# A third transposing bank, mirrors in threes and a regrouped step 0 in a graph-normalisation kernel on one Trainium2 core

## The reference

```python
def adjacent_mat(adj):
    adj = adj + jnp.eye(adj.shape[0])
    deg = jnp.sum(adj, axis=1)
    dinv = jnp.where(deg > 0, deg ** (-0.5), 0.0)
    return dinv[:, None] * adj * dinv[None, :]

S = adjacent_mat((A + A.T) * 0.5)
y = (A @ S) @ x
out = _layernorm(x + y, axis=-1)
```

## Time and profile before

| | us |
|---|---|
| median of 3 runs | 406.44 (406.38 to 407.13) |
| profiled execution, its own time | 406.92 |
| its span, first to last instruction | 405.1 |
| PE busy | 391.6 (97%) |
| DVE busy | 245.4 (61%) |
| ACT busy | 112.5 (28%) |
| POOL busy | 61.0 (15%) |

### The profile page before, as it was taken

How to read it: one execution, slowest core, us unless ns; L and a number is a source line. 1 busy time by engine, 2 the same in 40 slices (tenths; PEclk the granted TensorE clock), 3 DMA queues, 4 the chain that set the end, 5 groups by cost and what they waited for, 6 DMA issues and landing times.

```text
span 405.1 us, 5532 instructions
## 1 busy us (share of the span) xinstructions
PE 391.6 (97%) x1878; PEld 325.5 (80%) x1878; DVE 245.4 (61%) x477; ACT 112.5 (28%) x195; POOL 61.0 (15%) x95
## 2 busy tenths in 40 slices
PE   6989999999999999999999999999999999999994
PEld 5877787878888888888888888888888888888883
DVE  1887888865532622223663357777777778877742
ACT  1245455423332521112222212222222222221200
POOL 3455765732000000000000000000000000000000
PEclk9999999999999999999999999999999999999999
DMA  7999565431026762262322355555655666555300
GB/s 254 342 347 319 155 218 184 136 97 30 0 55 154 170 141 53 52 155 53 104 53 52 93 145 135 147 143 142 155 135 150 155 155 153 145 137 144 95 26 26
DMA packets 67889, 54.76 MB, mean 135 GB/s; under 512 B 3616, under 2 KB 56864, under 8 KB 67872
## 3 DMA queue, kind: packets, MB, share of 16 engines
q1 hardware_dynamic: 67872, 54.54, 50.5%
HBM read 41.94 MB, written 4.19 MB: 114 GB/s over the span
## 4 chain that ended last, share of the span: by engine, by line
issue 72%; PE 18%; DVE 4%; DMA 2%; POOL 2%; SPq 1%; ACT 0%; POOLq 0%; DVEq 0%; ACTq 0%
PE ps L424 4%; PE ps L426 4%; PE ps L425 4%; PE ps L447 3%; PE ps L455 2%; DMA lots_s<-adj 2%; POOL rstd L415 1%; DVE store L687 1%; DVE lots_s L687 1%; DVE c L716 1%; DVE col_acc L711 0%; DVE u_lo L746 0%; PE ps L468 0%; PE ps L436 0%; DVE c_lo L721 0%
## 5 line engine op out<-in xcount | busy, mean ns | idle before, releaser
L670 ACT ACTIVATE w_hi<-store 128x512 fp32r<-128x512 f32 x64 | 39.8, 631 | 122.9 <-DVE store L822 122.9
L424 PE MATMUL ps<-u_hi,w_hi 128*128 128x512 f32 x176 | 69.6, 395 | 0.0
L425 PE MATMUL ps<-u_lo,w_hi 128*128 128x512 f32 x176 | 68.5, 389 | 0.0
L426 PE MATMUL ps<-u_hi,store_lo 128*128 128x512 f32 x176 | 68.5, 389 | 0.0
L822 DVE STREAM_TRANSPOSE store<-store 128x512 f32<-128x512 f32 x64 | 65.5, 1071 | 0.0
L761 DVE SCALAR_TENSOR_TENSOR z_raw<-ps,dinv_half,z_raw 128x512 fp32r<-128x512 f32 x16 | 11.9, 751 | 73.2 <-ACT z_raw L625 73.2
L415 POOL TENSOR_TENSOR rstd<-var_eps,mhalf 128x1 f32<-128x1 f32 x16 | 8.8, 549 | 287.3 <-DVE var_eps L872 287.3
L424 PE MATMUL ps<-z,w_hi 128*128 128x512 f32 x128 | 49.8, 389 | 0.0
L425 PE MATMUL ps<-z,w_hi 128*128 128x512 f32 x128 | 49.8, 389 | 0.0
L426 PE MATMUL ps<-z,store_lo 128*128 128x512 f32 x128 | 49.8, 389 | 0.0
L424 PE MATMUL ps<-store_lo,w_hi 128*128 128x512 f32 x128 | 49.8, 389 | 0.0
(11 more groups left out here) (87 smaller groups left out, 566.5 us busy)
## 6 DMA issues: line engine op xcount, KB each, us to landing
store<-adj SPq DMA_DIRECT2D x65, 256.0 KB, 4.4
u_x<-x SPq DMA_DIRECT2D x16, 256.0 KB, 4.3
z<-z_raw SPq DMA_DIRECT2D x32, 128.0 KB, 2.3
store_lo<-z_raw SPq DMA_DIRECT2D x32, 128.0 KB, 2.3
x_res<-x SPq DMA_DIRECT2D x16, 256.0 KB, 2.6
out<-y_out SPq DMA_DIRECT2D x16, 256.0 KB, 2.0
lots_s<-adj SPq DMA_DIRECT2D x13, 256.0 KB, 4.0
col_slot<-adj SPq DMA_DIRECT2D x6, 448.0 KB, 8.4
```

The costliest lines, as they stand in the source:

```text
L424: nc.tensor.matmul(out_, hi, mov_hi, start=first, stop=False)
L425: nc.tensor.matmul(out_, hi, mov_lo, start=False, stop=False)
L426: return nc.tensor.matmul(out_, lo, mov_hi, start=False, stop=last)
L670: nc.scalar.activation(w_hi2(j)[:, CB * g:CB * g + CB], turned[j][:, CB * g:CB * g + CB], ACT.Copy).then_inc(s_hi2, 1)
```

## The change

- **Banks.** From step 1 on, T alternates between two banks, by a count that runs on over the steps. T(k,i) waits for add(k,i-2) and not for add(k,i-1). Mirrors get a third bank, the one that held the column sums; these keep the last quarter of it. So a mirror has at most three blocks (M counts from the end: 13 to 15, 10 to 12, ...).
- **Column sums.** `col_sums(k)` is now run just before M(k-1,1). ACT copies the result to SBUF (`store_sums`), after the store of M(k-1,1); M(k-1,2) and those behind it wait for that copy too, and so does `degrees(k)`.
- **DVE order.** `lot_low(k-1)` needs the first two mirrors now, and stands behind add(k,1); `u_low(k-1)` stands behind add(k,0). `first_low` 1 to 3 move from steps 2, 3, 4 to steps 5, 6, 8. `rest_high` and `rest_low` of the first rest panel are one step later.
- **Step 0.** Loads come in three parts (blocks 1 to 4, 5 to 11, 12 to 15). Warming transposes are 20, 19 and 20 (before 20 and 36). Column 0 is no longer made by four DVE additions: its blocks are mirrors of row 0, copied by ACT (`store_first`). The clearing of `col_acc` on POOL and the three additions of row 0 to it are replaced by three ACT copies (`first_sum`), one of 128x1280.
- **Loads of steps 1 to 4.** Each row comes in two pieces, the first four blocks early.

```diff
         def mirrors_of(k):
-            parts = [(i, max(b0, k + 1), b1) for i, (b0, b1) in enumerate(chunks_of(k)) if b1 > k + 1]
-            return parts[-1:] + parts[:-1]
+            ends = [(max(b - CB + 1, k + 1), b) for b in range(NB, k + 1, 1 - CB)]
+            return [(next(i for i, (c0, c1) in enumerate(chunks_of(k)) if c0 < b1 <= c1), b0, b1) for b0, b1 in ends]
...
-            return i % 2 if k < 2 else 0
+            return (chunk_at(k) + i) % 2 if k < NR else 0
...
+                for h, (b0, b1) in enumerate(((1, 5), (5, NR), (NR, NB))):
+                    sp.dma_start(c0[:, b0:b1], a_cols[0, :, b0:b1]).then_inc(s_in0[h], 16)
+                    if h == 0:
+                        sp.dma_start(c0[:, 0:1], a_rows[0, :, 0:1]).then_inc(s_in0[h], 16)
+                    sp.dma_start(row(0, b0, b1), a_rows[0, :, b0:b1]).then_inc(s_in0[h], 16)
...
-            nc.gpsimd.memset(col_acc[:], 0.0).then_inc(s_const, 1)
...
-                if main_part(k):
+                if k >= 1 and main_part(k):
                     pool.wait_ge(s_ul, k + 1)
                     pool.wait_ge(s_wlo, k + 1)
                     accumulate(k, *main_part(k), s_cb)
...
             def transpose_cols(k, i, b0, b1):
-                pe.wait_ge(s_add, chunk_at(k) + i - (k == 1 and i > 0))
+                pe.wait_ge(s_add, chunk_at(k) + i - (k < NR))
...
-            def mirror(k, n, i, b0, b1):
+            def mirror(k, n, i, b0, b1, with_sums):
                 pe.wait_ge(s_add, chunk_at(k) + i + 1)
                 if n:
                     pe.wait_ge(s_mir, n)
+                if with_sums:
+                    col_sums(k + 1)
+                else:
+                    pe.wait_ge(s_csr, k + (n > mirror_at(k)))
...
-            keep_busy(36)
+            keep_busy(20)
...
                 if 2 <= k <= NR:
                     u_high(k - 1)
                 if 1 <= k - 1 < NR:
-                    store_mirrors(k - 1, 1, NC)
+                    store_mirrors(k - 1, 1, 2)
+                if k >= 1:
+                    store_sums(k)
+                if 1 <= k - 1 < NR:
+                    store_mirrors(k - 1, 2, NB)
...
                     if 2 <= k < NR and i == 0:
+                        u_low(k - 1)
+                    if 2 <= k < NR and i == 1:
                         lot_low(k - 1)
-                    if 2 <= k < NR and i == 1:
-                        u_low(k - 1)
...
-                if 2 <= k <= len(FIRST):
-                    first_low(k - 1)
-                if NR - NC <= k < NR:
-                    rest_low(0, range(k - NR + NC, k - NR + NC + 1))
+                if k in FIRST_LOW:
+                    first_low(FIRST_LOW.index(k) + 1)
+                if NR - NC < k <= NR:
+                    rest_low(0, range(k - 1 - NR + NC, k - NR + NC))
```

More of the change, by code:

```diff
@@ L23, in build @@
     HALVED = 5
+    FIRST_LOW = [5, 6, 8]
     F = 4
@@ L426, in passes, with keep_busy @@
                 return nc.tensor.matmul(out_, lo, mov_hi, start=False, stop=last)
+            def keep_busy(n):
+                for _ in range(n):
+                    nc.tensor.transpose(idle, ident[:], ident[:])
             def first_step():
                 for i, (b0, b1) in enumerate(chunks_of(0)):
-                    if i in (0, 3):
-                        pe.wait_ge(s_in0[i // 3], 48)
+                    if i == 2:
+                        keep_busy(19)
+                    if i in (0, 2, 4):
+                        pe.wait_ge(s_in0[i // 2], 48 if i == 0 else 32)
                     if i >= 2:
@@ L434, in first_step, with mirror_first @@
                     for b in range(b0, b1):
-                        if i:
-                            nc.tensor.transpose(parked[i - 1][:, b - b0], row(0, b, b + 1)[:, 0], ident[:])
-                    for b in range(b0, b1):
                         last = nc.tensor.transpose(tp[i % 2][:, b - b0], c0[:, b], ident[:])
                     last.then_inc(s_tc, 1)
+                    if i >= 2:
+                        mirror_first(i - 1)
+                mirror_first(NC)
+            def mirror_first(i):
+                b0, b1 = chunks_of(0)[i]
+                pe.wait_ge(s_add, i + 1)
+                for b in range(b0, b1):
+                    last = nc.tensor.transpose(parked[i - 1][:, b - b0], row(0, b, b + 1)[:, 0], ident[:])
+                last.then_inc(s_tm0, 1)
             def transpose_cols(k, i, b0, b1):
-                pe.wait_ge(s_add, chunk_at(k) + i - (k == 1 and i > 0))
+                pe.wait_ge(s_add, chunk_at(k) + i - (k < NR))
                 if k > NR + 1:
@@ L497, in multiply_rest @@
                     last.then_inc(s_mm, 1)
-            def keep_busy(n):
-                for _ in range(n):
-                    nc.tensor.transpose(idle, ident[:], ident[:])
             pe.wait_ge(s_ident, 2)
@@ L592, in corner_high, with store_first, first_sum @@
                                      ACT.Copy).then_inc(s_mhi, 1)
+            def store_first(n):
+                act.wait_ge(s_tm0, n + 1)
+                b0, b1 = chunks_of(0)[n + 1]
+                nc.scalar.activation(c0[:, b0:b1], parked[n][:, 0:b1 - b0], ACT.Copy).then_inc(s_c0, 1)
+            def first_sum(b0, b1, signal):
+                nc.scalar.activation(col_acc[:, b0 - 1:b1 - 1], row(0, b0, b1), ACT.Copy).then_inc(signal, 1)
             def first_high(n):
```

87 lines of the change are left out of this document (50 added, 37 removed).

## The result

The changed kernel takes **413.27 us** (median of 4 runs, 413.14 to 413.64), beside 406.78 us for the kernel before on the same chip (406.38 to 407.14). The ratio is 1.0159, 95% interval 1.0147 to 1.0172: slower by 6.5 us. The forecast was 409.1 us and a range of 404.8 to 411.8. The sign was right, the size was 2.7 us where 6.5 came.

A forecast was written before the change was run, and what follows sets the result against it. PE, busy 97%, was taken as the bound, with the POOL, ACT and DVE loop at nearly its pace. Start -1.5, steps 2 to 4 +1.5, loop +2.7: 406.44 + 2.7 = 409.1 us, range 404.8 to 411.8.

The forecast's parts named there:

- loop from step 5 +2.7: From step 5 on, the POOL, ACT and DVE loop has longer turns and makes PE 2.7 us later.
- The start: Step 0 up to step 2: earlier warming, smaller first load and no additions to column 0 save 1.5 us.
- Steps 2 to 4: Waits for adds go, but mirror pairs in one bank and copies cost time: +1.5 us, spending the start's gain.
- The turn: One round of the POOL, ACT and DVE loop: long sum plus 4.35 us plus the add, 6.55 from row 4.
- rival 3: All worse: T(0,4) late by 0.4 us, disturbed short operations in every turn; 411.5 to 412.5 us, chance 0.08.
- The moved `first_low` 1 to 3 lie in DVE's wait for `u_high`: DVE: the moved subtractions, 0.8 to 0.95 us, hide in that wait.
- What PE makes of it: PE in step 9 waits for copies before mirror M(8,2); step 10 starts 2.6 us late, step 12 2.7.
- The clock is no term here: PE's granted clock is 1.00 in all stretches read, so it adds nothing to the sum.
- Past that PE has two rows of units in hand and no gaps now: From step 12 on, PE's lateness there stays the same to the end.
- Rival 1: POOL undisturbed: its short operations run at their short lengths; 406.9 to 407.9 us, chance 0.20 with its low end.
- Rival 2: PE's gaps go and the loop does not hold PE: 402.4 us, needing turns at or below 5.8; chance 0.15.
- The signs of being wrong: Long sum of row 9 starting before 76.5 us, or PE without waits for mirror copies from step 6 on.

The follow-up runs named there:

- e8: Kernel before, with POOL's clearing of `col_acc` moved behind the making of the identity; loads and order stay: 406.78 us.
- e4: Kernel before, with only DVE's swap: `u_low(k-1)` ahead of add(k,1) and `lot_low(k-1)` behind it: 414.57 us.
- e13: Changed kernel, DVE's order set back (`lot_low`, then `u_low`, both ahead of add(k,1)) only from step 5 on: 409.79 us.
- e7: Changed kernel, with `first_low` 1 to 3 put back into steps 2, 3 and 4: 412.55 us.
- e3: Changed kernel, with 12 idle transposes of the identity filling PE's wait ahead of the third mirror in step 9: 413.54 us.
- e2: Changed kernel, with PE multiplying the units that are left before the third mirror in step 9: 413.49 us.
- e1: Changed kernel, DVE's order set back in steps 2 to 11 (`lot_low`, then `u_low`, both ahead of add(k,1)): 412.17 us.
- e9: Kernel before, with the new step 0 alone (three load parts, row 0 mirrored and copied by ACT, first sums by ACT, no clearing): 405.99 us.
- e12: Changed kernel, POOL's long sums from row 4 on start without waiting for `u_low` and `lot_low`: 408.26 us.
- e11: Kernel before, POOL's long sums from row 4 on start without waiting for `u_low` and `lot_low`: 406.76 us.
- e6: Changed kernel, POOL's long sums in all rows wait for neither `u_low` nor `lot_low`: 409.49 us.

## Why the prediction was right or wrong

The step that failed is the term "loop from step 5 +2.7": the span grew by 6.3 us. It fell short in three places: the length of the turns (2.0 us), PE's lag behind the loop at step 12 (0.5) and the step behind it, which was to have no gap (0.8). These are 3.3 of the 3.6 us that were missing; the long sum of row 4 was 0.2 late already. The path was right, its operations were priced too low. In detail:

- **The start: right.** First unit at 15.46 (said 15.2), step 2 at 20.50 (said 20.7). The prediction counted POOL's clearing as a part of it (warming 1.6 us earlier); e8 shows that the clearing alone gives nothing with the old loads, and its share with the new ones stays open.
- **Steps 2 to 4: right in the sum, partly by luck.** Step 3 at 29.35 (29.2), step 4 at 37.24 (37.1), step 5 at 43.62 (43.7), step 6 at 49.91 (49.85); the long sum of row 4 at 48.45 (48.2). The start's gain is spent there, in waits at mirrors (0.63 us at each pair in one bank, 0.62 for the column sum's copy in step 3), as said. Step 2 also has 1.05 us at T(2,2), by elimination for a load, which the prediction did not have ("the loads ... still arrive ahead of use"); as step 3 came within 0.15 us all the same, something else in step 2 was priced too high.
- **The mechanism: right.** The loop over POOL, ACT and DVE becomes longer than PE's step because of `lot_low` behind `u_low`; e4 shows it alone (a turn of 6.59 where 6.55 was said), e13 takes most of it back.
- **The turn: the term that was mis-sized.** "Turns are thus the long sum plus 4.35 plus the add": the sum of five turns was 30.66 us and measured 32.69. The 4.35 was built from one turn of the kernel before, the one in the earlier trace rows, whose diagonal took 0.45. Of the missing 2.03 us, some 1.35 are three diagonals of 0.90 instead of 0.45 (turns of rows 4, 7, 8). Those of rows 4 and 7 run beside a moved `first_low`, and e7 made them short. In the turns of rows 7 and 8 the kernel before had diagonals of 0.90 and 0.91 too: they stood in its trace and were not in the sum. The turn of row 5 holds most of the rest: there the short sum started 0.59 us behind the long one, not 0.17. It started when DVE's `sum_lot` ended (56.56 to 57.61), which the long sum had held up; the program makes it wait only for the `sum_lot` of the row before, long done, so the two operations disturbed each other. These were told only as part of rival 3 ("disturbed short operations"), at 8%. The two diagonals of the kernel before, and the late short sum of the changed one:

```profile
66.96 0.90 POOL L411 TENSOR_TENSOR store<-store,ident 128x128 f32<-128x128 f32 x1
...
71.93 0.91 POOL L411 TENSOR_TENSOR store<-store,ident 128x128 f32<-128x128 f32 x1
```

```profile
57.66 0.75 POOL L393 TENSOR_TENSOR col_acc<-col_acc,store 128x128 f32<-128x128 f32 x1 [0.59 <-DVE col_acc L760]
```

- **"The moved `first_low` 1 to 3 lie in DVE's wait for `u_high`": wrong.** They lie beside POOL's short operations, which are the loop; the one of step 5 ends before DVE's wait for `u_high` begins. e7: 0.7 us.
- **What PE makes of it: wrong by 2.9 us.** Step 10 was to start 2.6 us late and started 5.5 late. M(8,2) came at 73.36, where 72.0 was said: 1.4 us of the late loop. From there to step 10 it took 3.8 us, where 2.2 was said: 1.6 us of slow matmuls, 0.43 us apart instead of 0.23. "The clock is no term here" was right for the sum only by luck: the granted clock did fall to 0.50, but e3 kept it at 1.00 and the time did not move.
- **What arrives at step 12** is the lateness of the loop at row 9: 5.3 us there (81.14 for 75.82, said 3.1), 5.4 at step 12 (86.81 for 81.41, said 2.7), and e2 and e3 come to the same 86.7 by other ways. In the kernel before, the changed one, and e1, e2, e3, e4, e7, e9 and e13, step 12 starts 5.3 to 5.8 us behind that long sum. So 2.2 of the 3.6 us that the sum lacked are the loop's, 2.0 of them the turns; 0.5 are PE's lag behind it (said 0.4 less than at row 9, measured 0.1 more), which no single wait was found for.
- **"Past that PE has two rows of units in hand and no gaps now": wrong by 0.8 us.** From step 12 on the sum was to stay; the unit of row 11 then waited for its `u_low`, 0.72 us (92.36), since DVE's chain was as late as PE; step 12 took 9.08 us for 8.25. The units in hand, of which the prediction spoke, are used up there:

```profile
92.36 0.50 PE L432 MATMUL ps<-u_hi,lots_r 128*128 128x512 f32 x1 [0.72 <-DVE u_lo L793]
```

- **Rivals.** Rival 1 (POOL undisturbed) did not come: the short sum was 0.63 to 0.75, not 0.46. Rival 2 (the loop does not hold PE) needed turns below 5.8; none was. Rival 3 had the right place, at 8% and 411.5 to 412.5, and would still have been low by 0.8. The signs of being wrong looked only to the low side ("long sum of row 9 before 76.5"); it started at 81.14, 2.2 later than said, and no sign covered that.

As a sum of what the experiments took away: start -1.0 (e9 against before, where it lasts); loop from row 4 on +5.0 (e12), of which `lot_low`'s place 3.5 (e13) and `first_low`'s about 0.7 (e7; these two may overlap). What is left, 408.26 (e12) against e11's 406.76 with the same free loop, is +1.5, or +2.5 with the start's gain: steps 2 to 4 are 1.2 us longer than in e11, steps 5 to 11 are 0.7, step 12 is 0.6. How much of the 1.2 is the mirror pairs, the order and the load was not separated; whether the last two come from the third mirror, from the copies of the column sums or from DVE's order was not tested.

## What to carry over

When the bound is a loop over several engines, take each of its operations over all its turns, not from the one turn that reads cleanly: the same operation had 0.45 and 0.90 us in one trace, and 0.45 us in each of three turns was a third of what the forecast missed. A subtraction that one engine does "while it waits" is free only if it neither stands ahead of something in the loop nor reads SBUF beside the short operations that the loop consists of; the cheapest way out here was to take the long operation out of the loop (it uses no data of the operations it waited for; the waits only kept them apart), and to do so only in the later rows: in all rows it gave 3.8 us (e6), from row 4 on 5.0 (e12). Before pricing an idle stretch or a slow clock, ask what comes last a few steps further on: taking away 1.35 us of idle time and the slow matmuls behind it was worth nothing.
